# Batch norm stage of a graph network kernel: finished rows turned by transposing DMAs instead of by TensorE

## The reference

```python
mu = jnp.mean(h, axis=0); var = jnp.var(h, axis=0)
h = (h - mu) * jax.lax.rsqrt(var + EPS) * gamma + beta
h = jax.nn.relu(h) + x                      # SAGE layer
x = _layernorm(x + h, axis=-1)              # so: layernorm(2 x + relu(bn(h)))
h = (x @ W).reshape(n, H, C)                # next layer, W: [512, 1024]
al_s = jnp.einsum('nhc,hc->nh', h, a_src)   # and 8 logits per node
```

## Time and profile before

| | us |
|---|---|
| median of 3 runs | 4247.26 (4243.65 to 4253.4) |
| the profiled execution | 4247.18, span 4245.5 |
| busy PE / DVE / ACT / POOL in the span | 3572.1 / 2165.2 / 1429.8 / 1455.5 |
| first product of the stage to its last output read | 1341.7 to 1828.4 |

### The profile page before, as it was taken

One profiled execution on the slowest core, in us unless ns is written; L12 is line 12 of the kernel. 1 busy time (PEld: TensorE's weight loads), 2 busy tenths in 40 slices (PEclk: granted clock), 3 DMA queues, 4 the chain that ended last, 5 costly groups with the idle time before them and its releaser, 6 DMA issues. The chain is left out here.

```text
span 4245.5 us, 59057 instructions
## 1 busy us (share of the span) xinstructions
PE 3572.1 (84%) x20056; PEld 2145.6 (51%) x20056; DVE 2165.2 (51%) x4085; ACT 1429.8 (34%) x2512; POOL 1455.5 (34%) x1188
## 2 busy tenths in 40 slices
PE   4589994599997999987599999998859999679733
PEld 3134441255554777765366666666635555234422
DVE  7167776433333444446643424213757887057576
ACT  1333333222222444344233323222534443323332
POOL 2455543322211222243433333213446665333111
PEclk7799996799998999999799999999979999789955
DMA  1767766543433556577876676744867675657587
GB/s 66 225 176 199 200 168 229 176 141 119 136 111 143 209 209 225 191 219 220 244 204 201 196 205 196 207 110 149 265 225 268 248 267 185 207 199 238 203 278 276
DMA packets 554428, 841.83 MB, mean 198 GB/s; under 512 B 288134, under 2 KB 288134, under 8 KB 552272
## 3 DMA queue, kind: packets, MB, share of 16 engines
q1 hardware_dynamic: 487120, 619.31, 44.4%
q0 software_dynamic: 67200, 221.25, 17.7%
HBM read 491.80 MB, written 284.56 MB: 183 GB/s over the span
## 5 line engine op out<-in xcount | busy, mean ns | idle before, releaser
L321 PE MATMUL bank<-w_lo,t_r_hi 128*128 128x344 f16 (+1 forms) x2560 | 837.1, 327 | 0.0
L322 PE MATMUL bank<-w_hi,t_r_hi 128*128 128x344 f16 (+1 forms) x2560 | 836.9, 327 | 0.0
L320 PE MATMUL bank<-w_hi,w_lo 128*128 128x344 f16 (+1 forms) x1280 | 418.7, 327 | 30.7 <-DMA w_lo<-g_row_lo 30.7
L2237 DVE SCALAR_TENSOR_TENSOR t_z<-w_lo,t_z 128x256 f32<-128x256 f32 x320 | 205.9, 704 | 440.3 <-DMA w_lo<-h 437.8
L320 PE MATMUL bank<-l_z_hi,w_lo 128*128 128x512 f16 x960 | 365.3, 381 | 1.5 <-DVE l_z_lo L1765 1.5
L321 PE MATMUL bank<-l_z_lo,w_hi 128*128 128x512 f16 x960 | 365.3, 380 | 0.0
L322 PE MATMUL bank<-l_z_hi,w_hi 128*128 128x512 f16 x960 | 365.0, 380 | 0.0
L2211 POOL TENSOR_TENSOR t_row_lo<-t_r,t_row_hi 128x1024 f16<-128x1024 f32 x80 | 181.3, 2267 | 517.0 <-ACT t_row_hi L2258 516.8
L1456 POOL DMA_INDIRECT l_z<-sum,slot_i x160 | 160.6, 1004 | 519.5 <-PE bank L1820 436.7
L320 PE MATMUL bank<-w_hi 128*128 128x344 f16 x960 | 297.7, 310 | 45.5 <-DMA w_hi<-t_row_lo 45.5
L322 PEld LDWEIGHTS bank<-w_hi,t_r_hi 128*128 128x128 f16 x2560 | 250.9, 98 | 168.3 <-issue 0.3
(11 more groups left out here) (277 smaller groups left out, 7031.7 us busy)
## 6 DMA issues: line engine op xcount, KB each, us to landing
w_lo<-h SPq DMA_DIRECT2D x160, 512.0 KB
h<-b_wide SPq DMA_DIRECT2D x80, 516.0 KB, 3.0
h<-w_hi SPq DMA_DIRECT2D x80, 516.0 KB, 3.2
sum_gat<-a_out SPq DMA_DIRECT2D x80, 514.0 KB
l_x<-x SPq DMA_DIRECT2D x40, 1024.0 KB
h<-l_h SPq DMA_DIRECT2D x40, 1024.0 KB
b_h<-h SPq DMA_DIRECT2D x40, 1024.0 KB
b_x<-x SPq DMA_DIRECT2D x40, 1024.0 KB
```

The costliest lines, as they stand in the source:

```text
L320: pe.matmul(out, s_lo, m_hi, start=(k == 0), stop=False)
L321: pe.matmul(out, s_hi, m_lo, start=False, stop=False)
L322: mm = pe.matmul(out, s_hi, m_hi, start=False, stop=last)
L2237: ins = v.scalar_tensor_tensor(out=z[u][:, s, cols], in0=hrow[:, s, cols], scalar=z[u][:, s, HC + h:HC + h + 1], in1=z[u][:, s, cols], op0 ...
```

## The change

- `turn_back` and the banks `tq` go. `high_parts` and `low_parts` work on rows: for each subtile of `o` they write `row_hi` and `row_lo` (one buffer each, four subtiles long). SyncE's `turn(g, s)` issues two DMAs that transpose a subtile of each (128x512) into `z_hi[u]`, `z_lo[u]`, which lie in the space of weights no longer used. There is one semaphore per subtile, `turned_in[s]`.
- `turn_rows` gets four banks and is done two groups ahead (g+2), in one piece after the products of subtile 0.
- ScalarE does `apply` for g+3 ahead of subtile 1 and `high_parts` for g+2 ahead of subtile 3. VectorE and GpSimd no longer follow a group ahead in their bodies; they are as far ahead as their waits let them.
- `wide` has four buffers, one per subtile.
- SyncE's loop over the groups is written out, in a new order: load `h` of g+4; then for each subtile `turn(g+1, s)` and the store of `wide`; the store of `o` of g+1 behind subtile 0 and the load of `x` of g+4 behind subtile 1.
- GpSimd's bias waits for `low_parts` instead of `turn_back`. `in_pairs` can leave more pairs out of the loop (`apart`).

```diff
     y = two("b_y", [P, S, D], F32) if not sage else [kn.buffer(mem, "b_y", [P, S, D], F32)] * 2
     o = two("b_o", [P, S, D], F32)
     if sage:
-        z_hi = kn.buffer(mem, "b_z_hi", [P, 2, 4, D], F16)
-        z_lo = kn.buffer(mem, "b_z_lo", [P, 2, 4, D], F16)
-        wide = two("b_wide", [P, GAT_ROW], F32)
+
+        row_hi = kn.buffer(mem, "b_row_hi", [P, S, D], F16)
+        row_lo = kn.buffer(mem, "b_row_lo", [P, S, D], F16)
+        dead = [w[:, 0:2 * S * 4 * P].rearrange("p (u a n) -> p u a n", u=2, n=P) for w in (kn.w_hi, kn.w_lo)]
+        z_hi, z_lo = ([w[:, u] for u in range(2)] for w in dead)
+        wide = [kn.buffer(mem, f"b_wide{s}", [P, GAT_ROW], F32) for s in range(S)]
     norm = Norm(kn, mem)
 
-    tp = [[kn.bank[n] for n in (0, 1, 0, 1)]] * 2 if sage else [kn.bank[0:4], kn.bank[4:8]]
-    tq = [kn.bank[2], kn.bank[3]]
+    tp = [kn.bank[0:4]] * 2 if sage else [kn.bank[0:4], kn.bank[4:8]]
     mm = [kn.bank[4 + n][:, 0:THIRD] for n in range(THIRDS)]
...
-    turned = pair("turned", 4 * H if sage else 0)
-    hi_done = take("hi_done", 4 * G if sage else 0)
-    lo_done = take("lo_done", 4 * G if sage else 0)
+    turned_in = kn.sig.several(S, "turned_in", 32 * G if sage else 0)
+    hi_done = take("hi_done", S * G if sage else 0)
+    lo_done = take("lo_done", S * G if sage else 0)
     prod = take("prod", THIRDS * S * G if sage else 0)
     wide_done = take("wide_done", THIRDS * S * G if sage else 0)
-    wide_stored = pair("wide_stored", 16 * 2 * G if sage else 0)
+    wide_stored = kn.sig.several(S, "wide_stored", 16 * G if sage else 0)
...
     def sync(sp):
-        def load(i, u):
+        def load_h(i, u):
 
             sp.wait_ge(rows_turned[u].sem, rows_turned[u].at(i * S))
             settle(sp, kn)
             sp.dma_start(h[u][:], dram["h"][:, :, ds(i * (2 * GROUP) + u * GROUP, GROUP)]
                          .rearrange("m p n -> p m n")).then_inc(h_in[u].sem, 16)
 
+        def load_x(i, u):
             sp.wait_ge(y_done[u].sem, y_done[u].at(i * S))
             sp.dma_start(x[u][:], node_rows(x_dram, i, u)).then_inc(x_in[u].sem, 16)
+
+        def turn(g, s):
+            u = g % 2
+            if g >= 2:
+                sp.wait_ge(prod.sem, prod.at((g - 1) * S * THIRDS))
+            sp.wait_ge(turned_in[s].sem, turned_in[s].at(g * 32))
+            for rows, done, out in ((row_hi, hi_done, z_hi), (row_lo, lo_done, z_lo)):
+                sp.wait_ge(done.sem, done.at(g * S + s + 1))
+                sp.dma_start(out[u][:, s * 4:(s + 1) * 4, :], rows[:, s, :], transpose=True)\
+                    .then_inc(turned_in[s].sem, 16)
 
         def store(i, u):
             if sage:
@@ -1935,39 +1949,57 @@
             sp.dma_start(node_rows(out_dram, i, u), o[u][:]).then_inc(stored[u].sem, 16)
 
         def group(i, u, last):
-            g = i * 2 + u
             if ahead(i, G):
-                load(i + 1, u)
+                load_h(i + 1, u)
+                load_x(i + 1, u)
             store(i, u)
-            if sage:
+
+        def store_wide(g, s):
+            sp.wait_ge(wide_done.sem, wide_done.at((g * S + s + 1) * THIRDS))
+            sp.dma_start(dram["h1"][g * GROUP + s * P:g * GROUP + (s + 1) * P, :], wide[s][:])\
+                .then_inc(wide_stored[s].sem, 16)
+
+        for g in range(2):
+            load_h(0, g)
+            load_x(0, g)
+        if sage:
+            for g in range(2, 4):
+                load_h(1, g - 2)
+                load_x(1, g - 2)
+            for s in range(S):
+                turn(0, s)
+            store(0, 0)
+            for g in range(G):
+                if g + 4 < G:
+                    load_h(*divmod(g + 4, 2))
                 for s in range(S):
-                    sp.wait_ge(wide_done.sem, wide_done.at((g * S + s + 1) * THIRDS))
-                    sp.dma_start(dram["h1"][ds(i * (2 * GROUP) + u * GROUP + s * P, P), :], wide[s % 2][:])\
-                        .then_inc(wide_stored[s % 2].sem, 16)
-
-        load(0, 0)
-        load(0, 1)
-        in_pairs(sp, G, group)
+                    if g + 1 < G:
+                        turn(g + 1, s)
+                    store_wide(g, s)
+                    if s == 0 and g + 1 < G:
+                        store(*divmod(g + 1, 2))
+                    if s == 1 and g + 4 < G:
+                        load_x(*divmod(g + 4, 2))
+        else:
+            in_pairs(sp, G, group)
         for u in range(2):
             sp.wait_ge(stored[u].sem, stored[u].at(16 * H))
-            if sage:
-                sp.wait_ge(wide_stored[u].sem, wide_stored[u].at(16 * 2 * G))
+        if sage:
+            for s in range(S):
...
 
         def low_parts(i, u):
             g = i * 2 + u
-            for k in range(4):
-                dve.wait_ge(hi_done.sem, hi_done.at(g * 4 + k + 1))
-                v.scalar_tensor_tensor(out=z_lo[:, u, k, :], in0=tq[k % 2][:], scalar=A_SCALE, in1=z_hi[:, u, k, :],
+            for s in range(S):
+                dve.wait_ge(hi_done.sem, hi_done.at(g * S + s + 1))
+                dve.wait_ge(turned_in[s].sem, turned_in[s].at(g * 32))
+                v.scalar_tensor_tensor(out=row_lo[:, s, :], in0=o[u][:, s, :], scalar=A_SCALE, in1=row_hi[:, s, :],
                                        op0=ALU.mult, op1=ALU.subtract).then_inc(lo_done.sem, 1)
 
         def group(i, u, last):
-            if not last:
-                residual(*following(i, u), range(S))
-                finish(*following(i, u))
-                low_parts(*following(i, u))
+            residual(i, u, range(S))
+            finish(i, u)
+            low_parts(i, u)
 
         def group_alone(i, u, last):
...
             finish(i, u)
 
-        residual(0, 0, range(S))
         if sage:
-            finish(0, 0)
-            low_parts(0, 0)
-        in_pairs(dve, G, group if sage else group_alone)
+            in_pairs(dve, G, group)
+        else:
+            residual(0, 0, range(S))
+            in_pairs(dve, G, group_alone)
 
     def scalar(act):
         def apply(i, u):
...
                 act.activation(h[u][:, m, :], h[u][:, m, :], func, scale=kn.bn_scale[:, m:m + 1],
                                bias=kn.bn_shift[:, m:m + 1]).then_inc(f_done[u].sem, 1)
 
-        def high_parts(i, u, chunks=range(4)):
-            for k in chunks:
-                act.wait_ge(turned[u].sem, turned[u].at(i * 4 + k + 1))
-                act.activation(z_hi[:, u, k, :], tq[k % 2][:], ACT.Copy, scale=A_SCALE).then_inc(hi_done.sem, 1)
+        def high_parts(i, u):
+            g = i * 2 + u
+            for s in range(S):
+                act.wait_ge(rows_out[u].sem, rows_out[u].at(i * S + s + 1))
+                act.wait_ge(turned_in[s].sem, turned_in[s].at(g * 32))
+                act.activation(row_hi[:, s, :], o[u][:, s, :], ACT.Copy, scale=A_SCALE).then_inc(hi_done.sem, 1)
 
         def group(i, u, last):
             g = i * 2 + u
             for s in range(S):
 
-                if s == 1 and ahead(i, G):
-                    apply(i + 1, u)
-
-                w = wide_stored[s % 2]
-                act.wait_ge(w.sem, w.at(g * 32 + (s // 2) * 16))
+                if s == 1 and ahead(i, G) and (u == 0 or ahead(i + 1, G)):
+                    apply(*following(i + 1, u))
+                if s == 3 and ahead(i, G):
+                    high_parts(i + 1, u)
+
+                act.wait_ge(wide_stored[s].sem, wide_stored[s].at(g * 16))
                 for n in range(THIRDS):
-                    if (s, n) in ((2, 2), (3, 1)) and not last:
-                        high_parts(*following(i, u), (0, 1) if s == 2 else (2, 3))
                     act.wait_ge(prod.sem, prod.at((g * S + s) * THIRDS + n + 1))
-                    act.activation(wide[s % 2][:, n * THIRD:(n + 1) * THIRD], mm[n], ACT.Copy, scale=UNSCALE)\
+                    act.activation(wide[s][:, n * THIRD:(n + 1) * THIRD], mm[n], ACT.Copy, scale=UNSCALE)\
                        .then_inc(wide_done.sem, 1)
 
         if sage:
             apply(0, 0)
             apply(0, 1)
             high_parts(0, 0)
-            in_pairs(act, G, group)
+            apply(1, 0)
+            high_parts(0, 1)
...
             pe.wait_ge(f_done[u].sem, f_done[u].at(i * 4 + 4))
             for s in subtiles:
 
-                if not sage:
+                if sage:
+                    pe.wait_ge(y_done[1 - u].sem, y_done[1 - u].at((i + u - 1) * S + s + 1))
+                else:
                     pe.wait_ge(y_done[u].sem, y_done[u].at((i - 1) * S + s + 1))
-                elif s >= 2:
-                    pe.wait_ge(y_done[u].sem, y_done[u].at(i * S + s - 1))
-                else:
-                    pe.wait_ge(y_done[1 - u].sem, y_done[1 - u].at((i + u) * S))
                 for m in range(4):
                     ins = pe.transpose(tp[u][s][:, m * P:(m + 1) * P], h[u][:, m, s * P:(s + 1) * P], kn.ident[:])
                 ins.then_inc(rows_turned[u].sem, 1)
 
-        def turn_back(i, u, chunks=range(4)):
```

(81 more changed lines are left out.)

## The result

The changed kernel takes 4355.57 us (median of 4 runs, 4346.1 to 4360.3) against 4247.23: ratio 1.025, 95% interval 1.0233 to 1.0268. It is slower by 108 us. The forecast was 77 us slower, 4324, with an inner range of 4300 to 4350 and a wide one of 4228 to 4360: the measured time is outside the inner range and 4 us inside the end of the wide one. The profiled execution took 4346.1 us.

What follows compares the result with a forecast made beforehand. TensorE bounds the batch norm stage; a new DMA loop takes 29.3 us per group against 24.5. Loop +76.8, tail -5.3, start +5.2 give +76.7 us: 4324 us, own range 4300 to 4350, 8 in 10 4228 to 4360.

Steps and rivals of the forecast that it cites:

- The bottleneck and the cover: Batch norm stage: TensorE alone sets the pace, 24.5 us per group, 22.75 without turn_back's transposes; DMA busy only 0.60.
- all hidden: Rival: batch norm stage takes 22.75 us per group with no wait at all, 4219 us; chance 0.10.
- The loop: Per group: TensorE's turning, load_h, queue, landing of turn(g+1,3), ScalarE's high part, next products; 28.6 us, 29.3 with clock loss.
- One sign: In the loop, ScalarE's b_row_hi was to wait for a turn DMA in 16 groups, longest at the fourth.
- The clock: TensorE's idling in each loop turn lowers the granted clock: 0.7 us per turn, between 0 and 1.05.
- The sum: Whole kernel: 76.8 us for 16 loop turns, -5.3 for the last groups, +5.2 at the start: +76.7 us.
- The tail: Groups 16 and 17, without loads, 23.7 us each; 18 and 19, 21.0 each; together -5.3 us.
- The start: Stage's start: TensorE's first product comes at 1346.9 instead of 1341.7, +5.2 us.
- Short transposes: Eight transposing DMAs of 128x512 per group take 0.61 us of queue each, 4.9 us per group (2.7 to 9.8).
- The loop is short: Rival: queue backlog does not build up, only the loop over wide 2 is left, 23.7 us per group, 4234 us; chance 0.12.
- Fast transposes: Rival: the eight transposes run at the plain rate, 2.7 us of queue, 27.1 per group, 4289 us; chance 0.12.
- Costlier short transposes: Rival: transposes take 8.1 us of queue instead of 4.9, 32.5 us per group, 4375 us; chance 0.05.

Runs made afterwards that it cites:

- e1: Changed kernel with ScalarE making the high parts of group g+1 ahead of subtile 1, instead of g+2's ahead of subtile 3: 4222.98 us.
- e2: Changed kernel with SyncE issuing the four turns of group g+1 at the list's start, ahead of the load of h: 4218.16 us.
- e3: Changed kernel with TensorE turning the rows of group g+2 before subtile 0's products instead of after them: 4249.65 us.
- e5: Changed kernel with plain DMA copies of the same bytes in place of the transposing ones, leaving out the turning: 4315.5 us.
- e6: Changed kernel with one more 1 MB transfer per group, the finished rows stored a second time right ahead of their store: 4410.25 us.
- e4: Changed kernel with 32 matmuls whose result nobody reads ahead of each group's products, to fill TensorE's idle time: 4343.39 us.

## Why the prediction was right

- *The bottleneck and the cover.* Right. Two reorderings (e1, e2) give 22.7 us per group, the 24.5 less 1.74 for the 16 transposes, and the time the prediction had for "all hidden", 4219.
- *The loop.* Right in every link. From the issue of `load_h` to the next group's first product it is 21.8 us as a mean; the prediction had 28.6 - 7.3 = 21.3. e1 cuts the loop at ScalarE, e2 at SyncE, e3 shifts its gate, e5 and e6 shorten and lengthen its content, each with the sign that it demands and, but for the 14 us of e3, nearly the size. One sign was off without effect: ScalarE's wait was to be longest at the fourth high part, and it is longest at the third (5.26 against 1.60 us), for the fourth's turn lands soon behind the third's.
- *The clock: the mis-sized term.* It was put at 0.7 us per group, at most 1.05, from the stage's start, where the lower level of 1.2 GHz lasted 2.1 us into the products. That was no measure of a loop turn, for the slow stretch had begun earlier there: TensorE had already been at its transposes from 1339.96, at 0.50, and only the rest of the stretch fell on products.

```profile
1339.96 1.96 PE L2067 MATMUL bank<-ident,b_h 128*128 128x128 f32 x8 [1.60 <-DVE b_z_lo L1998]
```

  In the loop TensorE does nothing for 5.0 to 7.1 us, and then the matmuls of the products start 0.29 us apart in place of 0.15 for 2.8 to 5.7 us, 4.0 as a mean over groups 1 to 15; in the group shown it is 5.2 (the row of 0.50 for 1438 to 1443 above). Half of the 4.0 is lost, 2.0 us. All of it lies ahead of SyncE's gate, so `load_h` goes out 9.26 us after the first product, and in e4 without the slow stretch 7.3.
- *The sum.* The stage grew by 107.9 us and not by 76.7. Of these 31.2, 28 are in the 16 turns of the loop (31.03 against 29.3): 20 by the clock (9.26 against 8.0 to the gate) and 8 behind the gate (21.77 against 21.3). 2 are in the tail and 1 at the start. So the forecast direction and mechanism were no luck, but its number is low by 31 of 108, mostly for one term.
- *The tail.* Groups 16 and 17, without loads, were to take 23.7 us each. The first `wide` stores of groups 16, 17 and 18:

```profile
1849.87 0.32 SPq L1959 DMA_DIRECT2D h<-b_wide  x1
...
1873.45 0.33 SPq L1959 DMA_DIRECT2D h<-b_wide  x1
...
1897.13 0.33 SPq L1959 DMA_DIRECT2D h<-b_wide  x1
```

  23.6 and 23.7 us. But group 16 still begins behind an idle time of 5.7 us, at the lower clock, which lies ahead of its first store: counted from first product to first product (1841.78, 1867.51, 1891.20) the two take 25.7 and 23.7.
- *The start.* +5.2 us forecast. Measured: first product 34.1 us after the stage's first issue (1345.27 - 1311.16) against 27.6 (1341.71 - 1314.12), +6.5.
- *Short transposes.* 0.61 us of queue each was about right. From the issue of `load_h` to ScalarE's last high part it takes 20.7 us as a mean (19.6 in the group shown); less the forecast's 1.1 + 13.6 + 0.5 for start, other data and landing, 5.5 are left, or 0.69 each (0.55 in the group shown). That is an estimate, as the 13.6 is the kernel before's. e5 puts the excess over a plain copy at 0.29; with the 0.33 of the plain rate that is 0.62. The lower rate of the row counted, not the one that the Trainium skill (Advanced Engine Details and Errata, section X-Bar Transpose (TRN2)) gives, by which transposes are as fast as regular DMAs: e5 would then have changed nothing.
- *The rivals.* "The loop is short" and "all hidden" are refuted by the period of 31.0. "Fast transposes" is refuted by e5: were they as fast as plain copies, the plain copies could not have saved 2.34 us per group. "Costlier short transposes" had 4375 us, nearer to the measured time than the forecast, but for another cause: it had 3.2 us more behind the gate, and there are 0.5.

## What to carry to other kernels

A DMA queue that is busy 60% of the time is not free room in any order: what counts is which transfers lie between a gate that the bottleneck engine opens and a landing that the same engine waits for. Before adding transfers, write down the loop from gate to landing, sum its content, and put work whose inputs are long ready ahead of the gate, or its consumer's wait behind the readings that free the bottleneck's buffers. An idle time per turn of a loop costs more than itself when the clock falls in it and the slow instructions lie ahead of the gate; take its size from a stretch that begins with the idle time, and from many turns rather than one.

## What the runs showed of the hardware

A short transposing DMA holds the engine that issues it for longer than a plain one. All 160 here were 128x512; the half that makes `z_hi` (columns: shortest, median, longest issue in ns; then issue to landing in us):

```profile
L1941 SPq DMA_TRANSPOSE w_hi<-b_row_hi x80: 1200/1620/2512, 1339.0 to 1908.1; - x80
...
DMA to landing us min/median/max: 2.5/5.6/8.6
```

1.2 us is the least per issue, for 4 blocks of 128x128, and the shortest issue of a plain copy of the same bytes took 0.46 (e5). In the queue behind other data a transpose cost 0.6 to 0.7 us (the estimates above), about half of its shortest issue; at the start, when the queue was short, the eight of group 0 took 11 us of SyncE (1338.98 to 1350.04).
